# Two transposes of a softmax's row maxima are issued later in the tick schedule of a two-layer transformer kernel

## The reference

```python
def _attn(q, k, v):                       # H = 16 heads of HD = 16
    scores = jnp.einsum('bhnd,bhmd->bhnm', q, k) * HD ** (-0.5)
    p = jax.nn.softmax(scores, axis=-1)
    return jnp.einsum('bhnm,bhmd->bhnd', p, v)     # then (b, n, 256)

h = _ln(x, ln1_w, ln1_b) * (1 + sc1) + sh1
q, k, v = jnp.split(h @ Wqkv + bqkv, 3, axis=-1)
x = x + _attn(q, k, v) @ Wos + bos
h = _ln(x, ln2_w, ln2_b) * (1 + sc2) + sh2
x = x + _attn(h @ Wq + bq, context @ Wk + bk, context @ Wv + bv) @ Woc + boc
h = _ln(x, ln3_w, ln3_b) * (1 + sc3) + sh3
x = x + gelu(h @ W1 + b1) @ W2 + b2
```

## Time and profile before

| | |
|---|---|
| median of 3 runs | 3849.95 us |
| profiled execution, its own time | 3849.95 us |
| its span | 3848.1 us |
| granted TensorE clock, mean | 0.991 |
| busy, TensorE | 3686.5 us (96%) |
| busy, VectorE | 2941.1 us (76%) |
| busy, GpSimd | 2576.1 us (67%) |
| busy, ScalarE | 2049.5 us (53%) |
| chain that ended last, TensorE's share | 75% |

### The profile page before, as it was taken

How to read it: one execution, slowest core, us unless ns; L and a number is a source line. 1 busy time by engine, 2 the same in 40 slices (tenths; PEclk the granted TensorE clock), 3 DMA queues, 4 the chain that set the end, 5 groups by cost and what they waited for, 6 DMA issues and landing times.

```text
span 3848.1 us, 94802 instructions
## 1 busy us (share of the span) xinstructions
PE 3686.5 (96%) x36086; PEld 3161.7 (82%) x36086; DVE 2941.1 (76%) x6006; ACT 2049.5 (53%) x6630; POOL 2576.1 (67%) x2579
## 2 busy tenths in 40 slices
PE   7999999999799999999999999899999999989999
PEld 6878877777699978888888887788888888879998
DVE  6888888888555578888888888889989898974443
ACT  4666666666433345555555555556555555553333
POOL 3565566665477766666666666677777777766776
PEclk9999999999899999999999999999999999999999
DMA  2111111112111237676767677677777777771111
GB/s 79 46 35 35 47 59 56 52 51 62 52 45 45 67 108 214 209 222 209 221 209 222 210 220 226 208 228 226 223 229 228 230 221 236 224 228 61 45 45 34
DMA packets 415201, 545.09 MB, mean 142 GB/s; under 512 B 58522, under 2 KB 311964, under 8 KB 414748
## 3 DMA queue, kind: packets, MB, share of 16 engines
q1 hardware_dynamic: 267224, 404.74, 31.9%
q10 hardware_dynamic: 147524, 134.30, 13.4%
HBM read 220.11 MB, written 184.55 MB: 105 GB/s over the span
## 4 chain that ended last, share of the span: by engine, by line
PE 75%; DVE 14%; ACT 3%; DMA 3%; issue 2%; ACTq 1%; POOL 1%; SPq 0%; DVEq 0%; POOLq 0%
PE BANKS L608 18%; PE BANKS L610 17%; PE BANKS L609 16%; PE BANKS L784 6%; PE BANKS L772 6%; PE BANKS L660 4%; DVE TOP L1072 3%; PE BANKS L723 2%; DMA p_scratch<-TR 2%; PE BANKS L834 2%; DVE HH L1025 2%; ACT HF L966 1%; DVE SN L1148 1%; ACTq L898 1%; DMA PB<-p_scratch 1%
## 5 line engine op out<-in xcount | busy, mean ns | idle before, releaser
L946 ACT ACTIVATE PR<-BANKS,NM 128x128 f32<-128x128 f32 x2048 | 721.2, 379 | 339.9 <-DVE NM L1134 339.8
L1275 POOL TENSOR_TENSOR PR<-PR,RL 128x512 f32<-128x512 f32 x512 | 533.7, 1042 | 341.2 <-DVE RL L1103 339.2
L608 PE MATMUL BANKS<-HH,WH 128*128 128x512 f32 x1632 | 688.4, 422 | 16.1 <-issue 6.3
L610 PE MATMUL BANKS<-HH,WL 128*128 128x512 f32 x1632 | 644.7, 395 | 0.0
L609 PE MATMUL BANKS<-HL,WH 128*128 128x512 f32 x1632 | 641.0, 393 | 0.0
L1134 DVE TENSOR_REDUCE NM<-BANKS 128x8 f32<-128x1024 f32 x256 | 310.2, 1212 | 190.8 <-PE BANKS L784 190.7
L946 ACT ACTIVATION_READ_ACCUMULATOR PR<-BANKS,NM 128x1 f32 x2048 | 445.6, 218 | 0.0
L1287 POOL TENSOR_TENSOR HL<-HF,HH 128x512 fp32r<-128x512 f32 x192 | 256.5, 1336 | 262.3 <-DVE HH L1026 164.6
L937 ACT ACTIVATE OH<-BANKS 128x512 fp32r<-128x512 f32 x256 | 153.2, 598 | 503.2 <-PE BANKS L772 271.6
L608 PE MATMUL BANKS<-WH,OH 128*128 128x256 f32 x1280 | 371.9, 291 | 27.2 <-DVE OL L1152 24.2
L608 PEld LDWEIGHTS BANKS<-HH,WH 128*128 128x128 f32 x1632 | 307.4, 188 | 109.8 <-issue 21.3
(11 more groups left out here) (133 smaller groups left out, 10068.2 us busy)
## 6 DMA issues: line engine op xcount, KB each, us to landing
SW<-SN SPq DMA_DIRECT2D x1024, 128.0 KB, 2.8
p_scratch<-TR SPq DMA_DIRECT2D x256, 512.0 KB, 4.9
PB<-p_scratch ACTq DMA_DIRECT2D x1024, 128.0 KB, 3.7
x_scratch<-X SPq DMA_DIRECT2D x80, 512.0 KB, 3.2
X<-x_scratch SPq DMA_DIRECT2D x80, 512.0 KB, 4.2
CX<-in_ctx SPq DMA_DIRECT2D x32, 384.0 KB, 3.6
X<-in_x SPq DMA_DIRECT2D x16, 512.0 KB, 3.7
out<-X SPq DMA_DIRECT2D x16, 512.0 KB, 2.9
```

Source lines behind the costliest of these rows:

```text
L608: e.matmul(o, lh, rh, start=first and i == 0, stop=False)
L610: made = e.matmul(o, ll, rh, start=False, stop=last and i == n - 1)
L946: made = e.activation(pr[:, r], bank[:, r], ACT.Exp, bias=nm[:, h:h + 1], accum_out=RL[npr(t)][:, h:h + 1])
L1275: e.tensor_tensor(p3, p3, RL[npr(t)][:, :].unsqueeze(2).broadcast_to([128, 4, 128]), ALU.mult).then_inc(s_nrm, 1)
```

## The change

`top_turn` moves from lag 3 to lag 5 and `top_out` from lag 4 to lag 5. In TensorE's program the loop of `top_turn` moves from behind the Z and context transposes to just behind `pv0`, ahead of q, k and v. In the planner of the banks its use moves in the same way.

```diff
-                for stage, lag in (("v", -3), ("v_out", -2), ("top_turn", 3), ("top_out", 4), ("pv0", 10), ("sums", 11), ("scale0", 12),
+                for stage, lag in (("v", -3), ("v_out", -2), ("top_turn", 5), ("top_out", 5), ("pv0", 10), ("sums", 11), ("scale0", 12),
                                    ("back", 13), ("high0", 13), ("low0", 14), ("out0", 15), ("res0", 16)):
@@ the planner of the banks
             for x in at["pv0", tick]:
                 tp.add(("pv", x), FOUR, s_to, 4 * xq(x.p, x.g) + x.b + 1)
+            for x in at["top_turn", tick]:
+                tp.add(("top", x), FOUR, s_m, 4 * xq(x.p, x.g) + x.b + 1)
...
-            for x in at["top_turn", tick]:
-                tp.add(("top", x), FOUR, s_m, 4 * xq(x.p, x.g) + x.b + 1)
@@ TensorE's program, behind pv0 (added) and behind c_turn (removed)
+                for x in at["top_turn", tick]:
+                    vi = 4 * xq(x.p, x.g) + x.b
+                    q.wait_ge(s_nm0, 2 * vi + 2)
+                    q.wait_ge(*tp.free(("top", x)))
+                    for c in range(2):
+                        made = e.transpose(PS[tp.bank(("top", x))][:, 128 * c:128 * c + 128], TOP[vi % 2][:, c, :], ID[:, :])
+                    made.then_inc(s_tt, 1)
```

More of the change, by code:

```diff
@@ L846, in _ @@
                     made.then_inc(s_turn, 1)
[L848 to L854, removed]
                 for p, g, j in at["up", tick]:
```

## The result

The changed kernel takes 3897.91 us, the median of 4 runs (3893.42 to 3906.59), against 3850.34 us before: 1.0124 times as long, 95% interval 1.0098 to 1.0148. The forecast was 3960 us: slower was right, the amount was 110 us and is 48. The profiled execution took 3895.49 us with a span of 3893.6, 45.5 more than before.

A forecast was written before the change was run, and what follows sets the result against it. Passes 0 and 1 were taken as bound by TensorE with short waits. Pass 0 11.7, pass 1 25.1 and the clock 73 sum to 109.8 us on 3849.95, forecast 3960 us, range 3868 to 3995.

The forecast's parts named there:

- The QM chain in the third batch: Pass 0: B (second score step) waits for transposes then QM, +0.53 us; +0.32 after the next A (first score step).
- the longer zigzag in the fourth: Pass 0, fourth batch: QM between maximum and OF makes OF, OH, HF, HH 1.15 us late; group 0.78 longer.
- The bank wait: Pass 1: second context transposes get a Z-transpose bank and wait 2.9 us for ScalarE's HF, in 16 groups.
- Pass 1 without the clock: Groups of pass 1 take 31.68 us against 30.11, +1.57 each, +25.1 us over 16 groups.
- the chain: Pass 1: the QM chain alone accounts for 0.64 us of each group's +1.57.
- the clock: Pass 1: the 2.9 us wait drops TensorE's granted clock in 13 of 16 groups, 5.6 us each, 73 us.
- The price: Each clock fall lasts until the next group's first 512-column products, 6.2 us of work at half clock, 5.6 us net.
- The first rival: Pass 1 wait shorter than 2.9 us, near 2.17, so the clock stays: 11.7 + 25.1, 3887 us; chance 0.22.

The follow-up runs named there:

- the filled wait: Changed kernel with the v product ahead of the context transposes' wait made five times into the same bank: 3883.55 us, 1.0096 of before.
- The run with the 4.2 us wait: Changed kernel with four extra ScalarE activations into an unused tile ahead of the second HF of the context groups: 3935.32 us, 1.0235 of before.
- TOP's bank: Changed kernel with the second context transposes given the bank of TOP in the same tick: 3872.99 us, 1.0069 of before.
- OF first: Changed kernel with OF (back) ahead of QM in VectorE's tick: 3877.68 us, 1.0087 of before.
- QM alone moved: Kernel before with only top_out at lag 5 instead of 4: 3859.92 us, 1.0040 of before.
- lag 4: Changed kernel with top_turn at lag 4 instead of 5, top_out still at 5: 3853.45 us, 1.0018 of before.
- lag 4 with OF first: Changed kernel with top_turn at lag 4 and OF ahead of QM on VectorE: 3849.75 us, 1.0008 of before.
- TOP's bank and OF first: Changed kernel with the second context transposes in the bank of TOP and OF ahead of QM: 3859.71 us, 1.0033 of before.

## Why the prediction was wrong

*Right, by its steps.* The QM chain in the third batch (+0.53 at B, here 4.00 - 3.40 = 0.60) and the longer zigzag in the fourth: 0.78 us a group in pass 0, measured 0.83, 12.5 us in 15 groups. From one A to the next the first and third batches are 0.37 us longer each (0.32 forecast), the second 0.05 shorter (nothing forecast) and the fourth 0.13 longer (0.14). The bank wait: 2.9 us forecast, 2.8 measured, at the instruction and for the semaphore named, 16 times. Pass 1 without the clock: 31.68 forecast, 31.53 measured, 1.53 x 16 = 24.5 us against 25.1. Of that 0.68 is the chain (0.64 forecast) and 0.85 the bank wait. Together 37.0 us, against 36.8.

*Wrong, by one term of the sum: the clock.* I put it at 13 groups of 5.6 us, 73 us. It is 8 groups, seven of 1.53 us and one of 2.8, some 13.5 us; the filled wait gave 10 to 14 back. Both factors are off.

The number: I read two single rows of other passes, 2.17 us that kept the clock and 2.88 that lost it, and took nearly all groups to be like the second. The table shows that the same wait at the same place costs the clock in some groups and not in others, from 2.0 to 3.2 us, and that 2.2 us, hardly more than the 2.17 that kept the clock in that row, does so in half of them. What divides the groups at one length, these runs do not settle. The trace before already held falls behind shorter waits, which I had not read: one at 2438.7, behind a wait of 2.06 us, and one at 988.0, where no single wait is longer than 1.7 us but several follow one another. The clock behind the wait of 2.88 us, and behind that of 2.06:

```profile
2425.00:2432.00 7.00, 6.13 (x15) 4.91 (x16) 5.08 (x7) 0.00 (x0) 2.81 (x3) 0.51 0.94 324
2438.00:2442.00 4.00, 3.95 (x34) 3.30 (x35) 0.48 (x1) 0.60 (x1) 1.72 (x2) 0.58 0.85 250
```

The price: I let the clock stay low until the next group's first 512-column products, 12.4 us, after one row of 13 us at the start of pass 0. In the changed kernel it is up again after 3.4 us, with scores, value and out products in that stretch. In the 13 us TensorE did mostly other work: scores and products of 64 columns for 8 us, and then the 512-column products, still at the low clock:

```profile
51.30 0.80 PE L608 MATMUL BANKS<-HH,WH 128*128 128x512 f32 x1
```

That one row was no measure of a stretch with other work in it, and the two windows above show shorter ones in the same trace: the fall behind the 2.88 us wait lasted 6.8 us, the one at 2438.7 3.4. Of 3.4 us at half the clock 1.7 should be lost and 1.53 are; where the last 0.2 goes no run shows. The run with the 4.2 us wait shows that the price holds when every group pays it, except where the clock stays low for 6.8 us.

The range, 3868 to 3995 us, holds the 3898, yet the forecast was more than twice the change. The first rival, bank wait without the clock at 3887 us, was the nearest, 11 us off, but not for its reason: the wait was not shorter than 2.9 us, it cost the clock in half of the groups, and each fall was cheap.

*The sum.* 12.5 + 24.5 + 13.5 = 50.5 us. At the start of pass 2 the changed trace is 49.5 us later than before, and at its end 45.5. The last 4 us lie in passes that the change does not touch. In the fourteen traces these passes take between 2832.2 and 2841.3 us, in no order with the edits, so a difference of a few us in the whole time says nothing. The first GF is the cleaner mark. Against the kernel before it is later by 22.1 us with TOP's bank, 36.7 with the filled wait, 27.5 with OF first, 11.1 with QM alone moved, 5.4 at lag 4, 3.1 at lag 4 with OF first and 10.7 with TOP's bank and OF first.

The Trainium skill, "Perfetto Trace Analysis", section Optimization Strategy, said of repeated gaps that PSUM may be short. The trace agrees that the gap is a wait for a bank, but the number of banks was not what made it: with the same four banks, handed out otherwise, the 2.8 us became 0.6. The Trainium skill's "TensorE: Matmul & The Clock Gate", section HAM oscillation, tells of a clock lost in every tile: at 4.2 us of wait that is so here in 16 of 16 groups, at 2.8 in 8.

## What to carry to other kernels

When a use is moved in a planner that hands out buffers in turn, list for every later use whose buffer it now gets, and on which engine's last reader it waits: here a move of two cheap transposes put another instruction behind the longest chain of the group. Put instructions whose result is needed soon ahead of long independent work, and not behind it; a transpose of 0.2 us behind a k product of 1.5 us (307.15 to 308.65 in the trace after) held the next step. Price a fall of the clock by how long it lasts behind work of the same kind, and test it by filling the wait with idle products.

## What the runs showed of the hardware

A granted clock that fell at the wait of the context transposes came back after 3.4 us in 46 of 53 falls (five runs) and after 6.8 in the other seven, while TensorE did scores, value products and 256-column products. A fall of 3.4 us cost 1.5 us. Whether a wait of 2.0 to 3.2 us costs the clock differs from group to group under the same work. The five executions of the changed kernel lie between 3893.4 us at a mean clock of 0.987 and 3906.6 at 0.984. Whether a different number of falls makes that difference isn't shown, since one of the five was profiled. And more work can be faster: five v products in place of one took 10 to 14 us off.
